# A fused attention and FFN kernel on one core: FFN layer one once per token as rows, mixed by VectorE for each cycle, layer four as columns, and the load phase in another order

## The reference, cut to what matters

```python
def _twist(x):
    o_r, o_i, p_r, p_i = jnp.split(x, 4, axis=-1)
    return jnp.concatenate([p_r, -p_i, -o_r, o_i], axis=-1)
gf = _global_net(x.mean(axis=1, keepdims=True), ...)       # one number per batch
out = x
for _ in range(3):                                         # NUM_CYCLES
    h = _gelu(out @ w1 + b1)                               # 256 -> 256, layer one
    h = _gelu(h @ w2 + b2)                                 # 256 -> 128
    h = _gelu(h @ w3 + b3)                                 # 128 -> 64
    tf = jax.nn.sigmoid(h @ w4 + b4)                       # 64 -> 1, layer four
    coupling = 0.1 + adaptive_range * (0.7 * gf + 0.3 * tf - 0.5) * 2.0
    out = out + coupling * _twist(out)
return out                                                 # then layernorm(x1 + out)
```

## Time and profile before

| what | value |
|---|---|
| median of three runs | 1787.38 us (1787.33 to 1787.47) |
| profiled execution | 1786.47 us |
| its span, first to last instruction | 1784.6 us |
| TensorE busy | 1733.3 us, 97% |
| VectorE, ScalarE, GpSimd busy | 1140.5, 743.8, 474.8 us |
| TensorE's granted clock over the span | 0.995 of 2.4 GHz |

### The profile page before, as it was taken

The page is one execution under the profiler, slowest core; times in us unless marked ns, Lnnn a source line. Parts: engine busy times, 40 slices in busy tenths (PEclk is TensorE's granted clock), DMA queues, the critical chain, the costliest instruction groups (busy, mean ns, idle before and its releaser), DMA issues.

```text
span 1784.6 us, 48313 instructions
## 1 busy us (share of the span) xinstructions
PE 1733.3 (97%) x21040; PEld 1300.8 (73%) x21040; DVE 1140.5 (64%) x2371; ACT 743.8 (42%) x1331; POOL 474.8 (27%) x373
## 2 busy tenths in 40 slices
PE   4999999999999999999999999999999999999996
PEld 3888888863588888885368888888447888888732
DVE  7667676755766666665586666666467666666645
ACT  3334342446542424345644333334564333333355
POOL 4323232311132323231232322222023232323202
PEclk9999999999999999999999999999999999999998
DMA  4000000000010000000010000000001000000001
GB/s 158 14 2 14 2 14 1 14 2 1 33 29 2 14 2 14 2 14 1 1 49 14 13 2 13 2 14 2 1 0 61 2 14 2 14 1 3 1 1 47
DMA packets 22834, 26.38 MB, mean 15 GB/s; under 512 B 3168, under 2 KB 21472, under 8 KB 22624
## 3 DMA queue, kind: packets, MB, share of 16 engines
q1 hardware_dynamic: 20624, 19.09, 3.4%
q10 hardware_dynamic: 2000, 4.20, 0.7%
HBM read 14.90 MB, written 8.39 MB: 13 GB/s over the span
## 4 chain that ended last, share of the span: by engine, by line
PE 88%; DVE 6%; ACT 3%; issue 2%; DMA 0%; POOL 0%; ACTq 0%; DVEq 0%; SPq 0%
PE bank L971 36%; PE bank L1051 10%; PE bank L1228 10%; PE bank L998 6%; PE bank L1038 6%; PE bank L1243 5%; PE bank L1015 4%; PE bank L1028 4%; PE bank L1007 3%; PE bank L1274 1%; PE bank L955 1%; PE bank L1259 1%; DVE att L787 1%; ACT q_sb L494 1%; DVE q_sb L709 1%
## 5 line engine op out<-in xcount | busy, mean ns | idle before, releaser
L398 POOL TENSOR_TENSOR k_end<-k_sc,pows 128x512 f32<-128x512 f32 x128 | 135.0, 1054 | 672.8 <-DVE k_sc L700 671.0
L837 DVE SCALAR_TENSOR_TENSOR h_seq<-h_seq,pows,bank 128x64 f32<-128x64 f32 x384 | 107.8, 281 | 273.3 <-PE bank L1015 262.3
L494 ACT ACTIVATE q_sb<-q_sb,pows 128x384 f32<-128x384 f32 (+2 forms) x384 | 167.6, 499 | 249.9 <-DVE q_sb L709 249.9
L510 ACT ACTIVATE h_sc<-h_seq,pows 128x256 f32<-128x256 f32 x128 | 65.3, 510 | 433.5 <-DVE h_seq L837 433.5
L407 POOL TENSOR_TENSOR o_lo<-o_g,o_hi 128x512 fp32r<-128x512 f32 x128 | 165.2, 1291 | 143.3 <-ACT o_hi L516 141.0
L787 DVE COPY_PREDICATED att<-causal,bank 128x1024 f32<-128x1024 int32 x128 | 167.9, 1312 | 0.5
L1051 PE MATMUL bank<-wo_hi,o_hi 128*128 128x256 f32 x512 | 149.3, 292 | 1.8 <-POOL o_lo L407 1.8
L516 ACT ACTIVATE o_hi<-o_g 128x512 fp32r<-128x512 f32 x128 | 81.1, 633 | 164.8 <-DVE o_g L803 164.8
L1051 PE MATMUL bank<-wo_hi,o_lo 128*128 128x256 f32 x512 | 144.3, 282 | 0.0
L1051 PE MATMUL bank<-wo_lo,o_hi 128*128 128x256 f32 x512 | 143.9, 281 | 0.0
L1038 PE MATMUL bank<-att,v_sb 128*64 128x128 f32 x2048 | 140.1, 279 | 0.6 <-DVE att L787 0.6
(11 more groups left out here) (143 smaller groups left out, 3771.5 us busy)
## 6 DMA issues: line engine op xcount, KB each, us to landing
x_in<-in_x SPq DMA_DIRECT2D x16, 512.0 KB, 4.1
out_y<-q_sb SPq DMA_DIRECT2D x8, 512.0 KB, 2.8
out_y<-x_nf SPq DMA_DIRECT2D x8, 512.0 KB, 3.0
v_sb<-in_wq ACTq DMA_DIRECT2D x1, 1024.0 KB, 5.1
v_sb<-in_wk SPq DMA_DIRECT2D x1, 1024.0 KB, 9.0
x1t<-in_wg ACTq DMA_DIRECT2D x1, 1024.0 KB, 9.3
x1t<-in_wv ACTq DMA_DIRECT2D x1, 1024.0 KB, 12.1
q_sb<-in_wo ACTq DMA_DIRECT2D x1, 1024.0 KB, 15.8
```

The costliest lines, as they stand in the source:

```text
L398: nc.gpsimd.tensor_tensor(k_end[:].rearrange("p (a z) (b r) -> p a (z b) r", z=2, r=BL), k_sc[:].rearrange("p (a z) (b r) -> p a (z b) r", ...
L494: last = nc.scalar.activation(q_sb[:, p % 2, d].rearrange("p (a z) n -> p a (z n)", z=2)[:, :, reach], q_sb[:, p % 2, 0].rearrange("p (a z ...
L837: step = nc.vector.scalar_tensor_tensor(h_seq[:, c + 1, :] if c + 1 < NC else h_st[:, p, :], h_seq[:, c, :], pows[:, p, HP + 1:HP + 2], ba ...
```

## The change

- **Layer one.** For tiles 0 and 1 (`rows_made`), each chunk of 128 tokens is the stationary operand and `f_w1`, now 512 columns wide (w1 beside the rows of w1 turned and signed as by the twist), the moving one: 2 matmuls of 512 columns give the layer's output for x1 and for twisted x1, tokens on partitions. ScalarE keeps them (`rows_kept`). For tiles 2 and 3 (`later_rows`) plain and twisted rows are 8 units of 4 matmuls of 256 columns, set between other layers and kept by VectorE. They are made once per batch, not once per cycle.
- **Per cycle.** VectorE mixes rows with one number per token: `second_rows`, `twisted_stepped`, `third_rows`, 4 instructions of 128x256 each per tile. TensorE turns the rows back to features on partitions (`rows_turned`, 16 small transposes), and ScalarE applies the gelu.
- **Layer four** gives one column per chunk: 8 products with a single moving column; tanh and the coupling are then on 128x8 numbers.
- **Order of visits**: (g, cycle) = (0,0), (0,1), (1,0), (0,2), (1,1), (1,2).
- **Final rows.** x1 + out is written as x1 and its twist with weights that GpSimd works out (`mix_begun`, `mix_ended`, 9 tiny instructions per group). After `final_transposed` ScalarE scales the rows from PSUM (`final_scaled`, 4 instructions), VectorE adds the twisted quarters (`final_summed`, 8), statistics read the sum from SBUF, and `final_normed` works in place. L926, L934, L453 and L633 are gone.
- **Next batch.** Values 0 to 7 (`coming_values`) are spread over the last two visits. For tiles 2 and 3 `final_scaled` and `final_summed` stand in head pairs 0 and 1, `final_stats` in 2 and 5, `final_normed` in 4 and 7. Each store is two DMAs instead of one, and stands behind the next load of x.
- **Load phase.** The order of weights is q, k, v, g. ScalarE's queue carries q, v, wo, issued after its first sigmoid, SyncE's carries k and g. VectorE makes all four low parts; GpSimd computes the powers; the gate product comes after value 3.

The core of the diff:

```diff
+                def rows_made(t, c):
...
+                    for k in range(KT):
+                        last = nc.tensor.matmul(z_bank(t, c), x1t[:, k, t * ST + c * C:t * ST + (c + 1) * C],
+                                                f_w1[:, k, :], start=(k == 0), stop=(k == KT - 1))
+                    last.then_inc(s_z, 1)
+                def rows_turned(v, j):
...
+                    if i:
+                        pe.wait_ge(s_zm, zm_done(b, g, i - 1, j))
...
+                    for k in range(KT):
+                        for c in range(NC):
+                            src = mixed(j, c) if i else z_plain(g * GT + j, c)
+                            last = by_halves(turn_bank(v, j), k * NC + c, src[:, k * P:(k + 1) * P])
+            def second_rows(b, g, j):
...
+                for c in range(NC):
+                    t = g * GT + j
+                    last = nc.vector.scalar_tensor_tensor(mixed(j, c), z_twisted(t, c), coupling_of(g, 0, t, c),
+                                                          z_plain(t, c), ALU.mult, ALU.add)
+            def final_scaled(b, t):
+                act.wait_ge(s_yt, b * NS + t + 1)
+                act.wait_ge(s_mix, (b * NG + t // GT + 1) * MIX)
...
+            def final_summed(b, t):
+                dve.wait_ge(s_fa, b * NS + t + 1)
+                for c in range(NC):
...
                             queries_of(p + 1, n + 1)
                             if p < 2 and s == 0 and b:
-                                final_stats(b - 1, p + 2)
+                                final_summed(b - 1, p + 2)
+                            if p in (2, 5) and s == 0 and b:
+                                final_stats(b - 1, 2 if p == 2 else 3)
...
                             tokens_of(n + 1)
...
+                            if p < 2 and s == 0 and b:
+                                final_scaled(b - 1, p + 2)
```

More of the change, by code:

```diff
@@ L303, in _ @@
             load_weight(sp, 1)
+            load_weight(sp, 3)
             for dst, src in consts:
@@ L639, in _ @@
+                layer2(b, 5, 0)
+                layer2(b, 5, 1)
+                layer3(b, 5)
+                layer4(b, 5)
+                final_normed(b, 0)
+                final_normed(b, 1)
+                if b + 1 == B:
+                    final_scaled(b, 2)
+                    final_scaled(b, 3)
+                    final_normed(b, 2)
+                    final_normed(b, 3)
         @block.vector
@@ L979, in project, with values @@
                                 lambda k: x_hi[:, k, :], lambda k: x_lo[:, k, :])
-            def values(it, m, first=0, end=6):
+            def values(it, m):
                 c, half = m // 2, m % 2
@@ new lines, in _ @@
+                for c in range(NC):
+                    rows_made(0, c)
+                rows_made(1, 0)
+                rows_made(1, 1)
+                rows_turned(0, 0)
+                rows_made(1, 2)
+                rows_made(1, 3)
+                x1_transposed(b * NS + NS - 1, 6)
+                rows_turned(0, 1)
+                layer2(0, 0)
+                layer2(0, 1)
+                global_net(1)
+                pe.wait_ge(s_x1c, (b + 1) * NS * KT + C0)
+                later_rows(2, 0, 0)
@@ new lines, in _ @@
+                global_net(2)
+                layer3(0)
+                global_net(3)
+                later_rows(2, 0, 1)
+                layer4(0)
+                later_rows(3, 0, 0)
+                rows_turned(1, 0)
+                later_rows(3, 0, 1)
+                rows_turned(1, 1)
+                layer2(1, 0)
+                layer2(1, 1)
+                rows_turned(2, 0)
+                layer3(1)
+                rows_turned(2, 1)
+                layer4(1)
+                layer2(2, 0)
@@ new lines, in _ @@
+                layer2(2, 1)
+                later_rows(2, 1, 0)
+                rows_turned(3, 0)
+                layer3(2)
+                later_rows(2, 1, 1)
+                rows_turned(3, 1)
+                layer4(2)
+                later_rows(3, 1, 0)
+                layer2(3, 0)
+                later_rows(3, 1, 1)
+                layer2(3, 1)
+                rows_turned(4, 0)
+                layer3(3)
+                rows_turned(4, 1)
+                layer4(3)
+                layer2(4, 0)
```

800 lines of the change are left out of this document (482 added, 318 removed).

## The result

The changed kernel takes 1794.59 us (median of 6 runs, 1794.03 to 1795.19) against 1787.45 of the kernel before on the same chip (6 runs): a ratio of 1.0036, 95% interval [1.0026, 1.0047]. It is slower by 7 us, 0.4%; the prediction was 1797.4. The profiled execution spans 1792.2 us, 7.6 more than before.

What follows compares the result with a forecast made beforehand. TensorE was taken to bound the FFN, VectorE's and ScalarE's chains the batch's edge and tail. Terms -9 + 4 + 15 + 5 - 5 = +10 gave 1796.5, plus 0.9 for the median 1797.4 us; range 1783 to 1808.

Steps and rivals of the forecast that it cites:

- FFN, -9: FFNs of batches 0 to 2: TensorE work -7.1, new waits +4.1, so -3.0 each, -9 us for three.
- Edge, +15: Start of next batch, head pairs 0 to 2: scaling and sums delay state steps and query products, +5 us each, three times.
- Last FFN, +4: Last batch's FFN, without value products as cover: less TensorE work but waits in full, +4 us (1 to 8).
- main case: The forecast itself, all terms summed without any rival: 1797.4 us, 0.56% slower, chance 0.44.
- rival 1: Edges and last FFN: TensorE's clock halves after waits, +1.4 us each, +8 to +12 in all, 1807; chance 0.13.
- Tail, +5: Last layer four to the end: ScalarE's and VectorE's chain grows from 18.5 to 23.6 us, +5 (3 to 7).
- Load, -5: Load phase: new weight order brings the first scores from 43.07 to near 38 us, -5 (-8 to +1).
- Rival 2: Load phase: GpSimd's chain of powers is locked out by VectorE, +1 in place of -5, 1803 us; chance 0.11.
- The +6: Load phase: sum higher by 6 us if shared-port locking let GpSimd's power links pass only between VectorE's low parts.
- Rival 3: Batch's edge: scaling and summing end before the next updates, edge costs 0 instead of +15, 1782 us; chance 0.16.

Runs made afterwards that it cites:

- e8: e7 plus eighteen value-product instructions nobody reads, filling TensorE's gaps in the last batch; 1774.53 us, ratio 0.9932 to the kernel before.
- e2: Changed kernel, with ScalarE in the last batch scaling tiles 2 and 3 before norming tiles 0 and 1; 1792.43 us, ratio 1.0021 to the kernel before.
- e3: Changed kernel with ScalarE's layer2(4,1) moved ahead of final_scaled(0) in each batch; 1789.25 us, ratio 1.0007 to the kernel before.
- e6: Changed kernel, load phase making the input's scaled, high and low parts before the key weight's high and low parts; 1792.57 us, ratio 1.0033.
- e4: Kernel before with only the new load phase (weight order, powers on GpSimd, low parts on VectorE); 1785.78 us, ratio 0.9986.
- e1: Changed kernel with the edge's transposes and scaled copies of tiles 2 and 3 moved earlier, nothing left out; 1783.19 us, ratio 0.9969.
- e5: Changed kernel with the edge's sums made for one chunk of four only, output incomplete; 1787.18 us, ratio 1.0002 to the kernel before.
- e9: e8 with the last coupling and its mix ahead of tile 1's statistics and power; 1774.01 us, ratio 0.9922 to the kernel before.
- e7: Changed kernel with the edits of e1, e2 and e3 together; 1774.98 us, ratio 0.9933 to the kernel before.

## Why the prediction was right

Slower was right, and by the mechanism named as deciding; the size was 3 us too high. That it came so close is in part luck: the rows of the ledger miss by 12 us when each counts in full, and the largest two misses, 4.7 too much at the edge and 2.6 too little in the last FFN, have opposite signs.

- *FFN, -9*: -10.1. Rows, later rows and turns came as their nearest rows said (14.0, 15.2, 8.3 against 13.9, 14.5, 8.5). The single columns took 0.99 a visit, near the 0.95 taken between 0.64 and 1.6. The half-width rows were under-booked: 32 x 0.87 / 2 is 13.9 and not 13.7, and they took 15.2. The waits, with the gaps round the value products, are 3.0, not 4.1; those at `rows_turned(1,0)` and `layer3(4)` are there, at 0.55 and 0.65 (1.0 and 1.4 forecast).
- *Edge, +15*: +10.3. This is the largest miss, 1.6 an edge. Head pair 1 lost 3.0 instead of 3.7, pair 2 0.95 instead of 1.0 (1.8, less the 0.8 for the statistics), and pair 0 became 0.5 shorter (10.38 against 10.92) where 0.3 of loss was booked. Two terms were mis-sized. The first is the chain ahead of the query product: it waited 1.87 and 1.51 where 2.5 and 2.4 were booked, and what waits behind it took 0.62 and 0.32 where 1.2 and 0.6 were. The scaled copies, given the norm's 1.91, took 1.57, and the sums 0.1 less than booked; the rest of the difference is not traced. The second is the start: the kept values, spread over the last two visits, come sooner and not later, and the old wait of 0.49 is gone.
- *Last FFN, +4*: +6.6. The wait at `layer3(4)` was 2.24 (2.8 forecast) and four others sum to 4.5. What was left out of the main case is the clock, which stood only in rival 1: at 0.50 for 12 us. Gaps filled in e8, the last visit is 2.3 us shorter. So rival 1 came true in the last FFN. At the edges it came true at one of the six waits for the query product in the changed kernel, one of 1.87 (two of six in e2, one in e3 and one in e6), and its price of 1.4 each was wrong there: head pair 1 lost 0.6 and pair 2 gave it back, and these edges are as long as the others (33.7).
- *Tail, +5*: +3.6. The chain was right. The first norm started 0.9 behind the last layer four where 2.0 was booked, and the copies took 2.98 for eight where 3.7 was taken. e2 shows that 2.8 of the 3.6 come only from ScalarE's order.
- *Load, -5*: -3.7 in the trace, -2.5 by e4's timing. The first product started 3.6 later than before (21.61 against 18.05) and not 1, which e6 shows to be of no account; the powers were there at 26.2, as booked. Rival 2's price was paid in part: links of 2.1 to 2.5 us in every trace. The Trainium skill, page "SBUF — State Buffer", section "SBUF: two separate sides", has the two engines share a port as a lock for a whole instruction; the row of 2.24 us beside VectorE's 2.29 agrees. The +6 that the prediction worked out from it did not come, since the chain needed only the time between the low parts for its other links.
- *Rival 3, the free edge, 1782*: it was wrong for the order given and right as a price. e1 makes the edge free by moving the same work, and takes 1783.19.
- *The rest, +0.9* is spread over the later head pairs (0.4, 0.1 and 0.4 in the three batches) and was not followed up. Executions differ by more than that for another reason, which is in neither of the two traces compared here. Ahead of the last FFN TensorE waits 1.79 us in every trace; in those of e2, e4, e5, e8 and e9 the clock fell to 0.50 behind it for some 3 us, in those of both kernels, e1, e3, e6 and e7 it did not. In e8 the stretch from that wait to the end of layer one is 1.6 us longer than in e7. Why the same wait drops the clock in some executions only stays open.
- *A check that did not hold:* the prediction has its fit of VectorE's steps (0.14 and 1.04 ns an element) agree with the state steps of 64 elements at 0.28 to 0.31. It gives 0.21 for them. Nothing was built on it, since the state steps were booked at their row.

What was not tried: the layer-four columns in another arrangement, the FFN part without the edge's new work in the kernel before, and the list order of e9 without the fill.

## What to carry to other kernels

Work that saves the bound engine time is paid for on the engines that prepare its operands: look in their lists for what stands ahead of a recurrence's step. Four copies and eight short sums cost 3.8 us a batch where the sums had to wait for the copies, and nothing once the copies were made earlier. When a stage has no filler work (the last batch), walk its chain again: waits that elsewhere hide show there in full, and the clock may go with them. And before paying for a faster engine in a tail, see which lists stand behind it: by the traces the fill was worth 0.4 us alone, and 1.8 once VectorE's and GpSimd's order was mended.

## What the hardware showed that was not expected

- Sixteen matmuls of one column with 64-row operands on alternating halves take 0.99 us, 0.06 each, about as long as layer four's four instructions of 512 columns in the kernel before (1.06).
- TensorE's clock fell to 0.50 after idle 2.24 and 0.79 us with 1.08 us of work between, in e3 already after 1.02 and 0.56. At the edges the same waits of 1.87 and 1.51, with some ten us of products between, left it at 1.00 in batches 1 and 3 and dropped it behind the 1.87 in batch 2. The Trainium skill, page "TensorE: Matmul & The Clock Gate", section "Part 1: The HAM clock gate", has the clock fall after idle time; these rows agree, and show that the length of the longest wait does not decide by itself: the same list with the same waits came out both ways.
- A slower TensorE clock can cost nothing: at the second edge 3.2 us at 0.50 made head pair 1 0.6 us longer, and the next wait for VectorE was shorter by as much.
- VectorE's copy of 128x64 takes 0.19 us, and 1.17 when it starts beside a GpSimd instruction that has 1.1 to go (e5).
- Four of ScalarE's scaled copies of 256 elements from a bank take 1.57 us; four norms of that size from a bank (scale and bias) took 1.91 in the kernel before, and eight from the x1t tile take 4.04 in the changed one.
